# Eight input transfers of a four-layer graph network begun on GpSimd's queue in place of ScalarE's

## What is computed

```python
def _L0_gnn_ref(h, adj, W_self, W_neigh):
    deg = jnp.clip(jnp.sum(adj, axis=1, keepdims=True), 1.0)
    h_neigh = adj @ h / deg
    return h @ W_self + h_neigh @ W_neigh

x = _layernorm(x + _L0_gnn_ref(x, adj, W_self, W_neigh))
x = _layernorm(x + _L1_gnn_ref(x, adj, kernel, bias))        # relu(adj @ (x @ kernel) + bias)
x = _layernorm(x + _L2_gnn_ref(x, adj, W1, b1, W2, b2))      # adj twice
x = _layernorm(x + _L3_gnn_ref(x, adj, W, b))                # adj twice
```

## Time and profile before

| what | value |
|---|---|
| median of three runs | 1135.65 us (1135.45 to 1136.23) |
| the profiled execution's own time | 1135.07 us |
| its span, first to last instruction | 1133.0 us |
| PE busy | 1125.5 us (99% of the span) |
| DVE, ACT, POOL busy | 839.9, 612.7, 78.0 us (74%, 54%, 7%) |
| transfers of `xt` from x transposed | 8, of 256.0 KB, begun by ACT, 6.5 us from issue to landing (median) |

### The profile page before, as it was taken

How to read it: one execution, slowest core, us unless ns; L and a number is a source line. 1 busy time by engine, 2 the same in 40 slices (tenths; PEclk the granted TensorE clock), 3 DMA queues, 4 the chain that set the end, 5 groups by cost and what they waited for, 6 DMA issues and landing times.

```text
span 1133.0 us, 14410 instructions
## 1 busy us (share of the span) xinstructions
PE 1125.5 (99%) x5068; PEld 910.7 (80%) x5068; DVE 839.9 (74%) x1046; ACT 612.7 (54%) x857; POOL 78.0 (7%) x50
## 2 busy tenths in 40 slices
PE   9999999999999999999999999999999999999998
PEld 4567878888888888888888888888888888888886
DVE  6899999999897667685545497656577555677996
ACT  1328555655844444564444474444366545566884
POOL 0001100010131111000000010000000000000121
PEclk9999999999999999999999999999999999999999
DMA  9988677667967666596666588666658665787993
GB/s 364 373 289 295 232 245 242 219 221 223 321 215 276 209 202 212 180 366 205 206 187 202 183 289 289 205 207 203 222 207 328 208 203 188 255 327 279 337 312 106
DMA packets 82644, 278.42 MB, mean 246 GB/s; under 512 B 8848, under 2 KB 14480, under 8 KB 82576
## 3 DMA queue, kind: packets, MB, share of 16 engines
q1 hardware_dynamic: 76000, 272.66, 70.7%
q10 hardware_dynamic: 6576, 4.85, 1.5%
HBM read 275.38 MB, written 2.10 MB: 245 GB/s over the span
## 4 chain that ended last, share of the span: by engine, by line
PE 92%; DVE 3%; issue 1%; POOL 1%; DMA 1%; ACT 1%; SPq 0%; POOLq 0%; DVEq 0%; ACTq 0%
PE acc L504 28%; PE acc L505 28%; PE acc L509 28%; PE acc L492 4%; PE acc L541 3%; DVE deg_part L801 2%; POOL rstd L962 1%; DMA raw<-adj_tiles 1%; DVE adj_lo L935 1%; ACT t_x L706 0%; PE acc L527 0%; PE acc L519 0%; ACT t_x L729 0%; DVE deg_part L798 0%; ACT t_aux L663 0%
## 5 line engine op out<-in xcount | busy, mean ns | idle before, releaser
L935 DVE TENSOR_TENSOR adj_lo<-raw,adj_hi 128x1024 fp32r<-128x1024 f32 x450 | 545.8, 1228 | 240.8 <-ACT adj_hi L776 225.5
L776 ACT CAST adj_hi<-raw 128x1024 fp32r<-128x1024 f32 x450 | 469.0, 1050 | 348.0 <-PE acc L509 316.4
L504 PE MATMUL acc<-adj_hi,op_hi 128*128 128x512 f32 x1398 | 551.3, 394 | 0.1
L505 PE MATMUL acc<-adj_hi,op_lo 128*128 128x512 f32 x1398 | 544.6, 390 | 0.0
L509 PE MATMUL acc<-adj_lo,op_hi 128*128 128x512 f32 x1398 | 430.7, 389 | 0.0
L509 PEld LDWEIGHTS acc<-adj_lo,op_hi 128*128 128x128 f32 x1398 | 262.4, 188 | 55.4 <-DVE adj_lo L935 0.2
L504 PEld LDWEIGHTS acc<-adj_hi,op_hi 128*128 128x128 f32 x1398 | 262.7, 188 | 54.2 <-issue 1.0
L505 PEld LDWEIGHTS acc<-adj_hi,op_lo 128*128 128x128 f32 x1398 | 262.7, 188 | 53.5 <-issue 1.0
L801 DVE TENSOR_TENSOR deg_part<-deg_part,raw 128x1024 f32<-128x1024 f32 x112 | 136.7, 1220 | 3.7 <-DMA raw<-adj_tiles 1.4
L962 POOL TENSOR_TENSOR rstd<-var_eps,minus_half 128x4 f32<-128x4 f32 x31 | 64.1, 2067 | 1038.0 <-DVE var_eps L817 768.8
L492 PE MATMUL acc<-raw,x_rows 128*128 128x512 f32 x176 | 78.3, 595 | 0.8 <-DMA raw<-adj_tiles 0.7
(11 more groups left out here) (82 smaller groups left out, 370.9 us busy)
## 6 DMA issues: line engine op xcount, KB each, us to landing
raw<-adj_tiles SPq DMA_DIRECT2D x515, 512.0 KB, 4.6
xt<-x_t ACTq DMA_DIRECT2D x8, 256.0 KB, 6.5
x_rows<-x_blocks SPq DMA_DIRECT2D x7, 256.0 KB, 9.2
out<-t_x ACTq DMA_DIRECT2D x7, 256.0 KB, 7.2
raw<-adj_tiles SPq DMA_DIRECT2D x2, 256.0 KB, 3.7
x_rows<-x_blocks ACTq DMA_DIRECT2D x2, 128.0 KB, 3.8
out<-xt SPq DMA_DIRECT2D x2, 128.0 KB, 1.8
w<-W ACTq DMA_DIRECT2D x2, 64.0 KB, 2.5
```

Of the source, the lines that this page charges most:

```text
L504: nc.tensor.matmul(bank, op_block(op_hi, p, j), a_hi, start=first and b == 0, stop=False)
L505: nc.tensor.matmul(bank, op_block(op_lo, p, j), a_hi, start=False, stop=False)
L776: nc.scalar.copy(split_hi(s), raw[:, g % RAW, :]).then_inc(hi_ready, 1)
L935: nc.vector.tensor_tensor(split_lo(s), raw[:, g % RAW, :], split_hi(s).bitcast(fp32), ALU.subtract).then_inc(lo_ready, 1)
```

## The change

All eight transfers of `xt` are begun by GpSimd. The first stands behind GpSimd's constants and waits for nothing but them. Transfer m + 1 stands ahead of chunk m's `rstd` in GpSimd's program and waits for `rows_done` to reach m + 1, the same condition as before. `xt_load` and its calls leave ACT's program. PE, DVE and SP keep their instructions in their order.

```diff
@@ self_rows (ACT)
                 act.wait_ge(rows_out, BPC * (m + 1))
                 nc.scalar.mul(row_mean[:], row_sum[:], -1.0 / D).then_inc(row_mean_ready, 1)
-                if m + 1 < CHUNKS:
-                    xt_load(m + 1)
@@ ACT
-            def xt_load(m):
-                if m > 0:
-                    act.wait_ge(rows_done, m)
-                act.dma_start(xt[:], cols(x_t, FINISH[m][1])).then_inc(xt_loaded, 16)
-
@@ ACT, after the third rounding of x
                         for dst, src in WEIGHTS[:2]:
                             act.dma_start(dst, src).then_inc(w_loaded, 16)
-                        xt_load(0)
@@ GpSimd
             pool.wait_ge(half_ready, 1)
+            nc.gpsimd.dma_start(xt[:], cols(x_t, FINISH[0][1])).then_inc(xt_loaded, 16)
             for m in range(len(NORM) * CHUNKS - 1):
+                if m + 1 < CHUNKS:
+                    pool.wait_ge(rows_done, m + 1)
+                    nc.gpsimd.dma_start(xt[:], cols(x_t, FINISH[m + 1][1])).then_inc(xt_loaded, 16)
```

## The result

The changed kernel takes 1138.69 us (median of 17 runs, 1136.67 to 1141.63), the kernel before, run beside it, 1135.34 us (median of 17). The ratio is 1.0023, with a 95% interval of 1.0015 to 1.003: slower by 1.7 to 3.4 us, 2.6 in the middle; the medians themselves lie 3.35 us apart. The range of 1134.4 to 1139.3 holds it, and the sign of the forecast was right, but +0.45 us had been forecast. The profiled execution is one of the longer ones, 1139.14 us with a span of 1137.0, 4.0 above the span before.

A forecast was written before the change was run, and what follows sets the result against it. PE, busy 1125.5 us or 99% of the span, was taken as the bound. Start +0.55, ACT's issues -0.10, waits 0 and queueing 0 gave +0.45 us: 1135.65 + 0.45 = 1136.1 us, range 1134.4 to 1139.3.

The forecast's parts named there:

- "same" 0.86: Chance of a time within 0.2% (2.27 us) of no change: the forecast 0.60 plus "nothing at the start" 0.26.
- the prediction's own last sign: Wrong in kind if PE idles over half a microsecond between 10 and 300 us, or the time is off by over 2.3.
- "They are 0.66 us of the engines' time ... I take 0.55.": At the start, the first transfer's bytes among the first tiles make PE late: +0.55 us, ends 0 and 0.66.
- "-0.10 us" from ACT's issues: ACT, rounding at 62.71 us: eight issues leave, 0.20 us hold goes, PE's wait for `op_lo` shrinks: at most -0.10 us.
- Seven transfers at cost 0: Seven transfers waiting on GpSimd in place of ACT arrive in time, even with 4.40 us for beginning one: cost 0.
- What queues behind the new waits: 0: On GpSimd only `rstd` queues; chunk 0's has 12.0 us against at most 4.40 for beginning the transfer: 0.
- DVE is held: Rival, 58 to 120 us: three GpSimd issues hold DVE 1.05 us each, 3.6 us with the start, 1139.25; chance 0.08.
- GpSimd is held: Rival: DVE starves GpSimd's beginning of transfer 3, PE waits 11.8 us for it from 114.09: 1147.9; chance 0.03.
- "From 9.20 us on it runs without a gap": PE's first steps: no gap after 9.20 us, so lateness there stays to the end, nothing behind being idle.

The follow-up runs named there:

- E11: Kernel before with two buffers for the last stores and the first transfer alone on GpSimd at 1.9 us, seven on ACT: 1136.99 us, ratio 1.0007.
- E12: Kernel before with two buffers for the last stores, all eight transfers on ACT, the first moved up to 1.7 us: 1136.72 us, ratio 1.001.
- E6: Kernel before with the last pass's stores taken in turn from two buffers, t_x and xt: 1135.35 us, ratio 0.999.
- E2: Changed kernel with the first transfer back on ACT at its old place, the other seven on GpSimd: 1136.16 us, ratio 1.0001.
- E3: Changed kernel, all eight transfers on GpSimd, the first held until PE has done six steps: 1137.35 us, ratio 1.0012.
- E7: Changed kernel with seven further 256 KB transfers into xt, read by nothing, begun by ACT in the third pass: 1138.73 us, ratio 1.0022.
- E9: Changed kernel with two buffers for the last stores and the first transfer held until PE has done six steps: 1136.29 us, ratio 1.0004.
- E5: Changed kernel with the last pass's stores taken in turn from two buffers, t_x and xt: 1137.01 us, ratio 1.0003.
- E10: Changed kernel with two buffers for the last stores and the first transfer back on ACT, seven on GpSimd: 1135.67 us, ratio 1.0001.
- E8: Changed kernel with the first transfer back on ACT, the other seven on SP's queue, none on GpSimd: 1135.7 us, ratio 0.9994.

## Why the prediction was right and wrong

The range held, the sign was right, and the mechanism of its only positive term was right. The size was not: +0.45 forecast, +2.6 measured, just above the 0.2% that I had taken for the bound of the measurable, where I had given "same" 0.86. That the range holds is luck: its upper end, 1139.3, stood there for a DVE that is held, which did not happen, and the late store, which did, stood nowhere. By the prediction's own last sign it was wrong in kind: 1138.69 is 2.6 us from 1136.1, and 2.3 was the limit.

- **"They are 0.66 us of the engines' time ... I take 0.55."** The term that was right in kind and mis-sized. The third step starts 0.88 us later. The bytes were priced at 400 GB/s, the rate of 6 to 12 us, but the transfer ran earlier. While it was on its way, 1.92 to 8.52 us, all transfers together reached 336 GB/s (q0 is GpSimd's queue, with this one transfer on it):

```profile
DMA packets 1031, 2.21 MB, mean 336 GB/s; under 512 B 114, under 2 KB 370, under 8 KB 1031
q0 software_dynamic: 80, 0.26, 12.4%
```

At that rate its 262,144 bytes are 0.78 us, and tile 2 came 0.81 us later; 0.66, kept as the upper end, was too low. Over many executions the start costs more than in this one profile, 1.2 us (E11) to 1.4 us (E12) by the median spans. Why it is more I can't say: the tiles' slack differs from execution to execution (E6's profile has no wait for the third step at all), but a lead of 0.45 us such as E6's is lost again at 125 us.

- **"-0.10 us" from ACT's issues.** Did not come. The rounding follows `row_mean` by 0.11 us (63.53 to 63.64) where it was 0.40 before, as forecast, but PE is not less late for it: 0.88 at 42 us, 0.97 at 264. `row_mean` itself waited 0.41 us and started 1.22 us later than before (62.31 to 63.53), so the rounding came 0.93 us later, as late as PE.
- **Seven transfers at cost 0.** Right for the waits: PE never waits for `xt`, and the bound of 4.40 us for beginning a transfer was far, it is 0.54 to 0.71. The whole cost is not 0 but 0.3 us, and it comes where the prediction did not look, in GpSimd's closing instructions at the end of the program.
- **What queues behind the new waits: 0.** Right; `rstd` of chunk 0 starts 11.1 us after GpSimd's issue ended.
- **DVE is held.** Did not happen: DVE's differences still take 1227 ns (1228 before), and E2's PE is late by 0.03 us at 264. The rule of the Trainium skill that I had set beside this rival ("SBUF — State Buffer", "Who interferes with whom": two-input vector instructions contend only with GpSimd instructions that read SBUF) agrees with the trace.
- **GpSimd is held.** Did not happen: landing 4.0 to 7.3 us. What the Trainium skill has against such transfers ("DMA: Bandwidth & Descriptors", "SWDGE vs HWDGE vs iDMA") does not show at the landing: the first transfer landed 6.6 us after its issue, between tiles of 5.3 and 7.3 us.
- **"From 9.20 us on it runs without a gap", and no look behind 300 us.** This is the step that failed. I looked for idle time of PE up to 300 us, found 0.11 us in all, and took the whole program as rigid, since no transfer of `xt` is used later. It is not: before the change the wait for the fourth store ended 0.3 us before ACT came for the buffer, and what the landing takes beyond 3.2 to 3.8 us goes straight to PE (6.0 less 2.3 here, 5.2 less 1.42 in E3, 4.5 less 1.26 in E7). A zero wait in the profile hid a slack of nearly zero. A fifth rival, "a late step in the last pass tips over", was missing from the list, and with 2.3 us in the profile and 1.7 between the medians it was worth more than the whole forecast.

What makes the store late stays open. It was late (4.5 to 6.0 us) in the profiles of the changed kernel, E3, E7 and E9 (4.8, where the second buffer hides it), and early (2.4 to 3.1) in the other ten. The four late ones all have eight transfers on GpSimd. Of the five kernels with eight only E5 was early, and of the nine others (seven in E2 and E10, one or none in the rest) not one was late. So the two go together in these profiles, one for each kernel; but the transfers ended 850 us earlier, and no mechanism is shown. E7 and E8 speak against ACT's queue as what it needs, E3 and E9 against the late start. Only a small part of the store is late. Of its 528 packets in the changed kernel, 39 lie behind 1097.1 us, 2.6 us after the issue, when the whole store of E5 or E6 has landed (whole store, then from 1097.1 us on):

```profile
q10 hardware_dynamic: 528, 0.26, 14.7%
...
q10 hardware_dynamic: 39, 0.02, 1.8%
```

Where the tile begun just before the store landed within 1.6 us of the store's issue, the store was mostly quick; E7 is an exception. The kernel before has long runs too: its median was 1136.37 on one chip and 1135.34 to 1135.38 on the others.

E6 is the kernel to keep: no slower than the kernel before (0.999, 0.9981 to 1.0), and without that lottery.

## What to carry to other kernels

A transfer that nobody needs for 40 us still costs its bytes if it is begun while the first tiles are on their way: begin it once the compute engine has work in hand. A wait that reads as zero in one profile may have a slack of 0.3 us; before calling a stretch rigid, compare for each late transfer the landing with the moment at which its reader comes. Follow the difference to the end of the span, behind the bounding engine's last instruction: 0.3 us of this change lay there. And look at single run times, not the median alone: two groups 1.5 us apart pointed at one wait.

## What the runs showed of the hardware that I had not expected

The same 256 KB store, from the same place in the program, lands in 2.4 us in one profile and 6.0 in another, with tiles of 512 KB before and behind it in both. At the start of the program, a transfer of 256 KB on a second queue delayed the tile on the first by 0.81 us, about what its bytes take at the 336 GB/s of that stretch (0.78). A transfer begun by GpSimd kept it for 0.54 to 0.71 us against 0.33 to 0.45 us on ACT, and landed no later (4.0 to 7.3 us, before 3.1 to 8.9). With seven or eight of them on GpSimd the program ended 0.3 us later behind its last store, or that store landed 0.7 to 0.9 us later.
